# Padding edge blocks to 256 in a graph-network kernel: one sum and one add per pair of chunks, one-hots four pairs ahead

## The reference

```python
agg = jax.ops.segment_sum(h[src], dst, num_segments=N)            # layer 0, and layer 2
a_in  = segment_sum(feat_in[src] * iw[:, None], dst, N)            # layer 1, edge weights
a_out = segment_sum(feat_out[dst] * ow[:, None], src, N)           # layer 1, the other direction
# layer 3: an MLP per edge, averaged over the edges of each node
#   hidden = relu(concat(x_dst, x_src - x_dst) @ W1 + b1); mean over edges, then @ W2 + b2
```

## Time and profile before

| what | value |
|---|---|
| median of 3 runs | 4508.78 us (4508.74 to 4520.75) |
| the profiled execution | 4500.45 us |
| its span (first to last instruction) | 4498.5 us |
| mean granted TensorE clock | 0.808 |
| busy: PE, PEld | 66%, 43% |
| busy: DVE, ACT, POOL | 55%, 34%, 57% |

### The profile page before, as it was taken

The page is one execution under the profiler, slowest core; times in us unless marked ns, Lnnn a source line. Parts: engine busy times, 40 slices in busy tenths (PEclk is TensorE's granted clock), DMA queues, the critical chain, the costliest instruction groups (busy, mean ns, idle before and its releaser), DMA issues. The chain is left out here.

```text
span 4498.5 us, 61024 instructions
## 1 busy us (share of the span) xinstructions
PE 2979.7 (66%) x12054; PEld 1939.9 (43%) x12055; DVE 2469.3 (55%) x6548; ACT 1514.4 (34%) x4772; POOL 2559.5 (57%) x2527
## 2 busy tenths in 40 slices
PE   0087886555558565555688875855555688999998
PEld 0033333333334333333466653333333346777775
DVE  8488885444343644444543444644444447777774
ACT  0177783100003310010111111400000147999994
POOL 3887776666661456666665565066666304555552
PEclk9999998666668666666688876966666789999999
DMA  2100003333340323333322223122222315666664
GB/s 84 30 2 2 2 2 90 89 88 89 86 87 1 105 80 89 87 86 85 91 84 82 80 85 75 49 90 86 86 89 87 51 55 161 183 183 179 181 180 127
DMA packets 171533, 390.02 MB, mean 87 GB/s; under 512 B 54847, under 2 KB 79398, under 8 KB 171483
## 3 DMA queue, kind: packets, MB, share of 16 engines
q0 software_dynamic: 127040, 331.70, 28.0%
q1 hardware_dynamic: 44443, 57.74, 3.9%
HBM read 361.22 MB, written 27.61 MB: 86 GB/s over the span
## 5 line engine op out<-in xcount | busy, mean ns | idle before, releaser
L643 POOL DMA_INDIRECT acc<-table,stg_idx x1680 | 1595.4, 950 | 965.5 <-issue 523.9
L1605 PE MATMUL psum<-acc,oh 128*128 128x257 f32 (+1 forms) x3360 | 1306.5, 540 | 1013.1 <-issue 380.1
L1605 PEld LDWEIGHTS psum<-acc,oh 128*128 128x128 f32 x3360 | 827.9, 267 | 1470.3 <-issue 1013.3
L1218 DVE TENSOR_TENSOR acc<-acc,psum 128x257 f32 (+1 forms) x1680 | 705.8, 420 | 1010.4 <-issue 482.3
L788 ACT COPY stg_lw<-rec 128x6 f32 (+1 forms) x840 | 164.7, 196 | 1980.1 <-PE psum L1605 1253.4
L633 POOL DMA_INDIRECT recs<-oh x400 | 512.8, 1282 | 194.9 <-issue 192.8
L710 POOL DMA_INDIRECT TT<-qtable,stg_row x420 | 398.6, 949 | 282.3 <-PE psum L1849 180.5
L1209 DVE TENSOR_SCALAR oh<-iota,stg_lw 128x128 f32<-128x128 f32 x1260 | 388.6, 358 | 310.6 <-issue 204.5
L1670 PE MATMUL psum<-H 125*128 125x420 bf16 x2000 | 401.6, 348 | 155.0 <-ACT H L742 118.5
L1849 PE MATMUL psum<-oh,TT 128*128 128x128 f32 x3360 | 434.3, 281 | 27.1 <-issue 16.6
L1849 PEld LDWEIGHTS psum<-oh,TT 128*128 128x128 f32 x3360 | 403.2, 193 | 95.2 <-issue 71.2
(11 more groups left out here) (195 smaller groups left out, 2700.3 us busy)
## 6 DMA issues: line engine op xcount, KB each, us to landing
acc<-table,stg_idx POOLq DMA_INDIRECT x1680
table<-H SPq DMA_DIRECT2D x12, 640.0 KB
TT<-loc_dram SPq DMA_DIRECT2D x21, 320.0 KB
TT<-qtable,stg_row POOLq DMA_INDIRECT x420
Wm<-loc_dram SPq DMA_DIRECT2D x21, 320.0 KB
recs<-oh POOLq DMA_INDIRECT x400
qtable<-H SPq DMA_DIRECT2D x24, 256.0 KB, 2.0
recs<-H SPq DMA_DIRECT2D x5, 840.0 KB, 11.3
```

Source lines behind the costliest of these rows:

```text
L643: pool.indirect_dma_start(out=dst[:, c, 0:D], out_offset=None, in_=src, in_offset=bass.IndirectOffsetOnAxis(ap=stg_idx[:, c:c + 1], axis=0 ...
L1218: V.tensor_tensor(at, at, sum_bank(c)[:, 0:w], ALU.add).then_inc(added, 1)
L1605: mm(sum_bank(c)[:, 0:w], oh[:, c, :], rowsbuf[:, c, 0:w], start=True, stop=True).then_inc(summed, 1)
```

## The change

A block's edges are padded to 256, so that both chunks of a pair belong to one block. The worst case becomes ITERS = 44, 440 chunks, 220 pairs. The two matmuls of a pair accumulate in one bank, of which five are used for the five pairs of an iteration, and VectorE adds a pair once. The block table has one entry for a pair, so half as many registers are loaded. LEAD goes from 2 to 4. In pass 4 the pair's sum accumulates in one of HB = 2 banks, and the one-hots move from ScalarE (`hot`, an absolute difference and a ReLU) to VectorE (`hot_rows`, one comparison for each chunk); ScalarE's `stage_rows` gets two waits for them. Counts that follow the number of chunks are changed with it (hi_ring 440 wide).

```diff
-ITERS = -(-(E + NB * (P - 1)) // (P * CH_IT))
+EDGES = 2 * P
+ITERS = -(-((E + NB * (EDGES - 1)) // EDGES) // SP_IT)
-SB = 5
-LEAD = 2
+SB = SP_IT
+HB = 2
+LEAD = 4
-            def hot(I, g):
-                j = g % SP_IT
-                act.wait_ge(summed, I * BODY + (4 * CHUNKS + 2 * g + 2))
-                for c in (2 * j, 2 * j + 1):
-                    last = nc.scalar.activation(oh[:, c, :], iota1[:, :], ACT.Abs, bias=stg_loc[:, col:col + 1], scale=1.0)
-                last.then_inc(near, 1)
-                act.wait_ge(near, I * CH_IT + g + 1)
-                nc.scalar.activation(t, t, ACT.Relu, bias=ones[:, 0:1], scale=-1.0).then_inc(hot4, 1)
-                    for d, do in ((1, relu), (4, turn), (2, hot)):
+                    for d, do in ((1, relu), (4, turn)):
                     if not last and g == SP_IT:
+                        act.wait_ge(hot4, I * CH_IT + SP_IT)
                         stage_rows(I * 2 + 2, 0)
                 if not last:
+                    act.wait_ge(hot4, I * CH_IT + CH_IT)
                     stage_rows(I * 2 + 3, 1)
-            def add_chunk(i, c, o, block0, w):
-                dve.wait_ge(summed, i * CH_IT + c + 1 + CH_IT)
-                dve.wait_ge(added, i * CH_IT + c + SB)
+            def add_pair(i, j, o, block0, w):
+                dve.wait_ge(summed, i * SP_IT + j + 1 + SP_IT)
+                dve.wait_ge(added, i * SP_IT + j + SB)
                 at = agg_flat[o][:, ds(block0, w)]
-                V.tensor_tensor(at, at, sum_bank(c)[:, 0:w], ALU.add).then_inc(added, 1)
+                V.tensor_tensor(at, at, sum_bank(j)[:, 0:w], ALU.add).then_inc(added, 1)
...
-                        for c in (2 * j, 2 * j + 1):
-                            add_chunk(i, c, d, first[c], pass_width(n))
+                        add_pair(i, j, d, first[j], pass_width(n))
...
+            def hot_rows(I, g):
+                j = g % SP_IT
+                dve.wait_ge(summed, I * CH_IT + (4 * PAIRS + g + 1))
+                for c in (2 * j, 2 * j + 1):
+                    col = g // SP_IT * CH_IT + c
+                    last = V.tensor_scalar(oh[:, c, :], iota1[:, :], stg_loc[:, col:col + 1], None, ALU.is_equal)
+                last.then_inc(hot4, 1)
...
+                    for do in (join, hot_rows):
...
-                for c in (2 * j, 2 * j + 1):
-                    pe.wait_ge(added, i * CH_IT + c + 1)
-                    mm(sum_bank(c)[:, 0:w], oh[:, c, :], rowsbuf[:, c, 0:w], start=True, stop=True).then_inc(summed, 1)
+                pe.wait_ge(added, i * SP_IT + j + 1)
+                for k in range(2):
+                    c = 2 * j + k
+                    last = mm(sum_bank(j)[:, 0:w], oh[:, c, :], rowsbuf[:, c, 0:w], start=(k == 0), stop=(k == 1))
+                last.then_inc(summed, 1)
...
-                for c in (2 * g, 2 * g + 1):
-                    pe.wait_ge(added, I * BODY + (4 * CHUNKS + SB - 4 + c + 1))
-                    for k in range(4):
-                        last = mm(hidden_bank(c)[:, k * P:(k + 1) * P], hbuf[:, c % CH_IT, k * P:(k + 1) * P],
-                                  oh[:, c % CH_IT, :], start=True, stop=True)
-                    last.then_inc(summed, 1)
+                pe.wait_ge(added, I * CH_IT + (4 * PAIRS + SB - HB + g + 1))
+                for k in range(4):
+                    for c in (2 * j, 2 * j + 1):
+                        last = mm(hidden_bank(g)[:, k * P:(k + 1) * P], hbuf[:, c, k * P:(k + 1) * P], oh[:, c, :],
+                                  start=(c == 2 * j), stop=(c == 2 * j + 1))
+                last.then_inc(summed, 1)
```

More of the change, by code:

```diff
@@ L23 @@
 CH_IT = 2 * SP_IT
-ITERS = -(-(E + NB * (P - 1)) // (P * CH_IT))
+EDGES = 2 * P
+ITERS = -(-((E + NB * (EDGES - 1)) // EDGES) // SP_IT)
 CHUNKS = ITERS * CH_IT
-SB = 5
-assert CH_IT % SB == 0 and EP * EC == E and CHUNKS % (2 * CH_IT) == 0 and CHUNKS % 4 == 0
-LEAD = 2
+PAIRS = CHUNKS // 2
+SB = SP_IT
+HB = 2
+assert EP * EC == E and CHUNKS % (2 * CH_IT) == 0 and CHUNKS % 4 == 0 and CH_IT % HB == 0
+LEAD = 4
 HID = 512
@@ L448, in block_starts @@
         def block_starts(eng, tab, size, row, first, count):
-            at = row * CH_IT + first
+            at = row * SP_IT + first
             return nc.values_load_multi_w_load_instructions(
@@ L706, in gather_hidden @@
                 for j in range(SP_IT):
-                    pool.wait_ge(summed, i * CH_IT + (4 * CHUNKS + 2 * j + 2))
+                    pool.wait_ge(summed, i * SP_IT + (4 * PAIRS + j + 1))
                     pool.sem_inc(stages_begun, 1)
@@ L783, in stage_pair @@
             def stage_pair(i, n, j):
-                act.wait_ge(summed, i * CH_IT + 2 * j + 2)
+                act.wait_ge(summed, i * SP_IT + j + 1)
                 c0 = (i - n * ITERS) * CH_IT + 2 * j
@@ L1224, in body @@
                 def body(i, last):
-                    first = block_starts(mybir.EngineType.DVE, agg_tab[o], S, i - n * ITERS, 0, CH_IT)
+                    first = block_starts(mybir.EngineType.DVE, agg_tab[o], S, i - n * ITERS, 0, SP_IT)
                     for j in range(SP_IT):
@@ L1237, in sum_pass @@
                 iterations(dve, n, body, len(between))
-                dve.wait_ge(added, (n + 1) * CHUNKS + SB)
+                dve.wait_ge(added, (n + 1) * PAIRS + SB)
             def gin_input(st, col):
@@ L1492, in add_hidden @@
             def add_hidden(I, g, blocks):
-                for c in (2 * g, 2 * g + 1):
-                    dve.wait_ge(summed, I * BODY + (4 * CHUNKS + CH_IT + c + 1))
-                    dve.wait_ge(added, I * BODY + (4 * CHUNKS + c + SB))
-                    at = H[:, :, ds(blocks[c], P)]
-                    V.tensor_tensor(at, at, hidden_bank(c).rearrange("p (k n) -> p k n", k=4), ALU.add).then_inc(added, 1)
+                dve.wait_ge(summed, I * CH_IT + (4 * PAIRS + SP_IT + g + 1))
+                dve.wait_ge(added, I * CH_IT + (4 * PAIRS + g + SB))
+                at = H[:, :, ds(blocks[g], P)]
+                V.tensor_tensor(at, at, hidden_bank(g).rearrange("p (k n) -> p k n", k=4), ALU.add).then_inc(added, 1)
+            def hot_rows(I, g):
[5 more added lines that the diff above has]
+                last.then_inc(hot4, 1)
+            dve.wait_ge(staged4, 1)
+            dve.wait_ge(p_ready, NB)
+            dve.wait_ge(p_hi, NB)
+            hot_rows(0, 0)
+            hot_rows(0, 1)
             join(0, 0)
@@ L1507, in body4 @@
                         add_hidden(I, g - 1, blocks)
-                    if g + 2 < CH_IT:
-                        join(I, g + 2)
-                    elif not last:
-                        join(I + 1, g + 2 - CH_IT)
+                    if g + 2 == SP_IT:
+                        dve.wait_ge(staged4, I * 2 + 2)
+                    if not last and g + 2 == CH_IT:
+                        dve.wait_ge(staged4, I * 2 + 3)
+                    for do in (join, hot_rows):
+                        if g + 2 < CH_IT:
+                            do(I, g + 2)
+                        elif not last:
+                            do(I + 1, g + 2 - CH_IT)
                 add_hidden(I, CH_IT - 1, blocks)
@@ L1516, in _ @@
             body4(ITERS // 2 - 1, True)
-            dve.wait_ge(added, 5 * CHUNKS + SB)
+            dve.wait_ge(added, 5 * PAIRS + SB)
             def finish_rows(t):
@@ L1558, in chunk_table @@
                 dst = take_bank(f"table{o}", 1)
-                done(mm(dst[0:96, 0:CHUNKS], ones[0:NB - 1, 0:96], ends_ge, start=True, stop=True), f"table{o}", 1)
+                done(mm(dst[0:96, 0:PAIRS], ones[0:NB - 1, 0:96], ends_ge, start=True, stop=True), f"table{o}", 1)
             def transpose_group(layer, g):
@@ L1612, in pass_end @@
             def pass_end(n):
-                pe.wait_ge(added, (n + 1) * CHUNKS + SB)
+                pe.wait_ge(added, (n + 1) * PAIRS + SB)
             def products(st, n, nf, terms, k0=0):
@@ L1647, in down @@
                     products(st, n, 2, [(w[:, k, :], H_at(k, n)) for k in range(nk)], n * 2)
-            pe.sem_inc(summed, CH_IT)
+            pe.sem_inc(summed, SP_IT)
             pe.sem_inc(spread, 2)
@@ L1871, in _ @@
             body4(ITERS // 2 - 1, True)
-            pe.wait_ge(added, 5 * CHUNKS + SB)
+            pe.wait_ge(added, 5 * PAIRS + SB)
             for n in range(NT):
```

59 lines of the change are left out of this document (26 added, 33 removed).

## The result

The changed kernel takes 4594.75 us (median of 4 runs), the kernel before 4508.76 us in the same set of runs: a ratio of 1.0188, interval 1.0166 to 1.021, so it is slower by 86 us, clear of the noise. I had forecast 4363 us, faster. The profiled execution spans 4592.4 us.

A forecast was written before the change was run, and what follows sets the result against it. POOL's gather pace plus its waits for ScalarE, and ScalarE in pass 4, were taken as bounds. Gather passes -117, pass 4 -34, edge placing +5 make -146 on 4500.45; adding 8 gives 4363 us, range 4220 to 4560.

The forecast's parts named there:

- The bound: Gather passes: POOL issues a gather every 1.25 us, a floor of 525 us a pass; waits for ScalarE add 433.3 us.
- the +100 us: Gather passes: 20 more gathers in each of four, 80 x 1.25 us, which nothing hides.
- Fewer additions, longer lead: Gather passes: VectorE's steps per pair fall from 12 to 7, so 0.5 of POOL's 433 us wait stays, -217 us.
- the stalls stay: Rival, gather passes: POOL freed sooner spends more time in VectorE's slow regime, share of stalls unchanged; +92, 4601 us, chance 0.17.
- wait above 360 us: Sign that the forecast is wrong: POOL's wait for ScalarE in passes 0 to 3, expected to fall from 433 to 217 us.
- Pass 4: ScalarE falls to about 1.9 us a pair, TensorE's 2.71 becomes the limit; 685 to 651 us, -34.
- Slow steps: Rival: in pass 4 POOL's runs lengthen and VectorE, now carrying one-hots, slows; +85 in place of -34, 4482 us, chance 0.17.
- The one-hots held POOL up: Rival, pass 4: VectorE's one-hots add 0.48 us to POOL's 2.50 a pair; +26, 4423 us, chance 0.04.
- they add nothing: Pass 0: beside VectorE's one-hots (0.48 us for two) gathers still come every 1.25 us, so no time is added to POOL's.
- the trace does not agree: Claim that, for these one-hots, the trace contradicts the skill's rule that VectorE's two-port mode locks GpSimd out of its port.
- Placing the edges: Edge-placing stage: 20 more TensorE matmuls of 420 columns, 19 us of work, mostly hidden; +5 us, between 0 and 19.

The follow-up runs named there:

- set 3: Later runs on one chip without the long stops: kernel before, unchanged, 4049.7 us; changed kernel, unchanged, 4139.0 us, ratio 1.0221.
- the drain: Changed kernel in which POOL, after every 10 gathers of the gather passes, waits until its last pair has landed: 4688.6 us, ratio 1.0377.

## Why the prediction was wrong

**The bound.** POOL's 1.25 us a gather as the floor was right, and so were the +100 us: 101.5 measured in set 3. The whole price of the 20 chunks was 176 us, because they count in pass 4 too (within my sum there) and because each pass has a longer tail of unused chunks, which I had not priced.

**"Fewer additions, longer lead" is the step that failed.** It was to give -217 us and gave some -30: above 1.25 us a gather the passes of the kernel before hold 436 us, those of the changed kernel 407. With the +100 that makes the 70 us by which they got longer, where I had -117. (POOL's row of waits for ScalarE falls by more, from 433.3 to 364.1, but some of its stops stand under another name then.) I took VectorE's register operations of 700 ns, which fall in the same stretches as the waits, for their cause. In the changed kernel they are gone, all of them, and most of the stops are left; the lead halved changes next to nothing; and in set 3 the kernel before has neither. What holds POOL is TensorE's signal that reaches ScalarE and VectorE together, 5 to 9 us after the matmuls, most often when POOL has gathered for 15 us or more. That a run cut at 12.5 us meets few of them (the drain) is shown; what delays the signal is not.

**The rival "the stalls stay"** gave 4601 us, and that it came so near is luck: it had +121 us for the passes, measured +70, and -34 for pass 4, measured +17. Its mechanism, slow steps that persist, is as wrong as mine. My indicator "wait above 360 us" was set to catch this and did, at 364.1. I gave it 0.17; having written that the reason for the slow steps "isn't in the trace", I had no ground for nearly three times that chance on their cure.

**Pass 4** was the second miss, of 51 us. Limit and size were right where the signals are in time (set 3): TensorE at 2.71 us a pair, 2.80 with all losses, 27 us less for the pass where I had said 34. In the run that was predicted they are late, and the pass is 17 us longer, not shorter: POOL still waits 159.2 us for the sums (180.5 in the earlier trace rows), and 20 chunks more go through. Slow steps did not reach pass 4. The one-hots held POOL up by under 2 us in set 3; "they add nothing" was nearly right in size, but "the trace does not agree" was wrong: I had compared gathers that had started ahead of the one-hots. The earlier trace rows had the sign of it, two one-hots that take 0.59 us at 1021.76.

**Placing the edges**, +5: the first gather starts at 724.3 us in place of 722.9. Within its bounds, and of no weight.

**Sum.** Without the stops: merge -26, move of the one-hots about -60, lead 0, the 20 chunks +176, together +90; measured 4139.0 - 4049.7 = +89. Each of these is the difference between one version and the next, so that they add up is no further proof. With the stops it is +86 at first measurement, 92 us off for the version of 42 iterations and about 175 on for the chunks. The totals are alike, the parts are not. From the kernel before to 42 iterations, the passes with their tails lose 64 us with the stops and 31 without (2574.0 to 2509.9, 2166.5 to 2135.2, first gather to last sum), pass 4 loses 20 and 62 (681.2 to 661.4, 640.8 to 578.6). So the merged pairs and the lead did win a part of the stops back, and the late signals took most of what the move of the one-hots gives.

## What to carry to other kernels

Where one engine issues at a fixed pace, as POOL here at 1.25 us a gather, count its instructions first: here 5% more of them cost more than all that was saved beside them. Take the 20 chunks out, with the blocks still padded to 256, and the rest of this change is a gain of 2.2%, the best version here (42 iterations, 3962.9 us), good for a graph whose blocks fit in 420 chunks. Two things that happen in the same stretch need not be cause and effect; look for two idle engines that start at the same instant, and ask which signal both waited for, and run the unchanged kernel again before building on a wait whose cause the trace does not name.

## What the runs showed of the hardware

The kernel before took 4509 and 4519 us (medians) in two sets of runs and 4048 to 4052 in three others, with the same 0.81 mean clock in the traces of both; the difference lies in the stages in which POOL gathers. A long set and a short one carry the same chip number, 15; what the reason is stays open. In the long ones TensorE's semaphore reaches the engines that wait for it late, by 5 to 9 us in the stop shown, and several increments at once; 524 of the changed kernel's 880 additions are over 2 us late, against 7 in a short set. VectorE's register operations of the kernel before took 0.7 us in stretches there, those of the changed kernel never. A one-hot of VectorE that starts some 0.4 to 0.6 us into a gather takes up to 0.51 us in place of 0.28, and a gather that starts within a one-hot up to 1.07 us in place of 0.94. Gathers whose 128 rows are all the same one seem to land every 1.65 us and not every 1.25. Two fills of 0.1 us between gathers, waited for, cost 1.25 us, and six 2.4 us.
